# Attention values of four heads in one group every second step, output sums copied by VectorE in the even steps

## The chip, the cores and the metric

The kernel runs on one core of one Trainium2 chip. The metric is the device time of one launch in microseconds (us), as the median of several runs.

## What is computed

One decoder layer, all in float32: self-attention with a causal mask, attention over a context with a mask of its own, and a mixture of experts. Cut to the part that the change touches and what follows it:

```
# x: (2, 256, 256), context: (2, 512, 256), 16 heads of 16, 16 experts, top 4
scores = einsum('bqhd,bkhd->bhqk', Q, K)            # causal: -inf above the diagonal
attn   = softmax(scores)
out    = einsum('bhqk,bkhd->bqhd', attn, V)
x = x + out @ Wo.T + bo
x = x + context_attention(layernorm(x), context, mask)   # zero where no position of the mask is valid
x = x + experts(layernorm(x))
```

## The kernel before

The program is written by hand: each engine has its own instruction list, and semaphores tie the lists together. What follows names TensorE PE, VectorE DVE, ScalarE ACT and GpSimd POOL, as the profile does.

Self-attention runs as a pipeline over 16 steps, v = 0 to 15 (`NV = 16`), and two more that drain it. A step is a pair of heads of one sequence. Two steps make a group `u` of four heads; groups 0 to 3 are the first sequence, 4 to 7 the second. In step v each engine does, in this order:

- **PE**: `scores(v)` (lines 1095 and 1099), then `turn(v-1)`, which transposes the exponentials of the step before (line 1109, three transposes for each of the two heads, each head behind a wait on `exp_done`). In odd steps from 3 on comes `values_first(u)` with u = (v-3)/2 (line 1122): four matmuls of 32 rows of output and 256 queries, over the first block of keys. In the next, even step, after `turn`, comes `values_second(u)` (line 1129), four matmuls over the second block of keys, which ends the sums of the group and increments `av_done`. In two steps, 9 and 17 (`LAST_VALUES`), both parts stand together in the odd step. In the trace each of these f32 matmuls is two instructions, so four are shown as x8.
- **DVE**: in odd steps from 5 on, and in step 10, it first copies the sums of a finished group out of PSUM bank 6 into `osum` (line 812, increments `o_done`). Then it takes the row maxima of the two heads (line 819, four instructions and a short read of the accumulator after each), then copies the first head's transposed exponentials from PSUM to `pt` (line 838). After that stand small pieces of other work: two maxima of the context's mask into `valid` in steps 7 and 8 (line 847); the attention outputs of the first sequence, `outputs` (lines 744 and 745), in steps 10 and 11; `residual` (lines 751 and 657) in steps 12 and 13; `centre` (lines 759, 761, 763) in step 14.
- **ACT**: the exponentials of the step, four activations (line 515), which wait for the maxima, then the second head's copy to `pt` (line 564).

Around the middle other work stands on PE: `turn_back(0, 0)` at the end of step 10 and `turn_back(0, 1)` in step 11 (line 1137), which transpose `osum` of the first sequence back and wait for `o_done` of 4 and, the second, for `att_done`; transposes of `att` (line 1007) at the end of step 11; `project` (line 1146) in step 12; transposes of `xn` in step 15; `context_scores` (line 1158) in steps 16 and 17. POOL makes `pen` (lines 366 and 369) from the mask once both `valid` columns are there, and behind it, on the same engine, the first `rstd` (line 312), which waits for `centre`.

Since `values_first(u)` overwrites the bank that the copy to `osum` reads, it waits for `o_done` of u. PE's `scores(v)` use PSUM banks 2(v mod 3) and the next, so three steps are in flight.

Of the kernel before, what the change touches and what calls it, by code (L numbers as in the profile page):

```python
# [15 lines left out]
B, S, D = 2, 256, 256  # L16
# [10 lines left out]
NG = H // HG  # L27
# [16 lines left out]
def decoder_layer(nc, x_d, ctx_d, ctxT_d, wqkv_d, wo_d, params_d, rows_d, mask_d, dbias_d, we_d, out_d):  # L44
    ctx = ExitStack()
    with ctx:
        def sb(name, shape, dt=F32):
            return ctx.enter_context(nc.sbuf_tensor(name, shape, dt))
# [4 lines left out]
        PS = ctx.enter_context(nc.psum_tensor("PS", [P, 8, 512], F32))  # L53
# [52 lines left out]
        osum = sb("osum", [P, NG, T])  # L106
# [85 lines left out]
        av_done, o_done = sem("av_done"), sem("o_done")  # L192
# [20 lines left out]
        NV = 2 * B * NG  # L213
        Q_BANK = (2, 7)
        TAIL = 2 * NG + 3
        LAST_VALUES = (2 * NG + 1, 4 * NG + 1)

        block = ctx.enter_context(nc.Block())

# [426 lines left out]
        def _(dve):  # L646
            v_ = nc.vector
# [156 lines left out]
            for v in range(NV + 2):  # L804
                if v == 0:
                    dve.wait_ge(causal_done, 2)
                if v == 2 * NG + 2 or (v >= 5 and v % 2 == 1 and v != 2 * NG + 3):
                    u = NG - 1 if v == 2 * NG + 2 else (v - 5) // 2
                    b, hg = divmod(u, NG)

                    dve.wait_ge(av_done, u + 1)
                    v_.tensor_copy(osum[:, hg, b * S:(b + 1) * S], PS[:, 6, 0:S]).then_inc(o_done, 1)  # L812
                if v < NV:
                    for j in range(2):
                        dve.wait_ge(sc_done, 2 * v + j + 1)
                        if v >= 2:
                            dve.wait_ge(exp_done, 2 * v + j - 3)
                        for qc, cols in ((0, slice(0, P)), (1, slice(P, BLK * P))):
                            i = v_.tensor_tensor_reduce(out=masked[:, v % 2, j, cols], in0=PS[:, 2 * (v % 3) + j, cols],  # L819
                                                        in1=causal[:, cols], scale=1.0, scalar=HUGE, op0=ALU.add, op1=ALU.min,  # L820
                                                        accum_out=nmax[:, v % 2, j, qc:qc + 1])
                        i.then_inc(max_done, 1)

                if v == NV - 1:
                    low_tokens(7, yh_done, 1, slice(0, S), yl_done)
                if v == NV:
                    context_scale(0)
                    dve.wait_ge(pen_done, B)
                    context_max(0)
                if v == TAIL:  # L830
                    outputs(0, 1, 7)
                if 1 <= v <= NV and v != NV - 2:

                    w = v - 1
                    dve.wait_ge(pT_done, 2 * w + 1)
                    if w >= 4:
                        dve.wait_ge(av_done, w // 2 - 1)
                    v_.tensor_copy(pt[:, w // 2 % 2, 2 * (w % 2), :, :].rearrange("p c q -> p (c q)"),  # L838
                                   PS[:, 2 * (w % 3), 0:BLK * P]).then_inc(pt_done[0], 1)
                if v == 1:  # L840
                    take_queries(1)
                if v == 5:
                    take_values(1)
                if v in (7, 8):
                    b = v - 7
                    dve.wait_ge(mask_in, 16)
                    v_.tensor_reduce(valid[:, b:b + 1], mask8[:, b * M:(b + 1) * M], AX.X, ALU.max).then_inc(valid_done, 1)
                if v == TAIL - 1:
                    outputs(0, 0, 7)
                if v == TAIL + 1:  # L850
                    dve.wait_ge(xb_done, 1)
                    dve.wait_ge(proj_done, QC)
                    residual(0, 0, PS[:, 7, 0:D])
                if v == TAIL + 2:
                    residual(0, 1, PS[:, 7, D:2 * D])
                if v == TAIL + 3:
                    centre(0)
# [141 lines left out]
        def _(pe):  # L999
# [109 lines left out]
                        i = t.transpose(PS[:, 2 * (v % 3) + j, n * P:(n + 1) * P], pr[:, v % 2, j, n * P:(n + 1) * P], ident[:, :])  # L1109
                    i.then_inc(pT_done, 1)  # L1110

            def values_first(u):

                b, hg = divmod(u, NG)
                if u % NG == 0:
                    pe.wait_ge(v_done, QC * (b + 1))
                for j in range(2):
                    pe.wait_ge(pt_done[j], 2 * u + 2)
                if u >= 1:
                    pe.wait_ge(o_done, u)  # L1120
                for h in range(HG):
                    t.matmul(PS[HP * h:HP * (h + 1), 6, 0:S], vp[:, b * QC, hg * HG + h, :],
                             pt[:, u % 2, h, 0:QC, :].rearrange("p c q -> p (c q)"), start=True, stop=False, skip_group_check=True)

            def values_second(u):

                b, hg = divmod(u, NG)
                for h in range(HG):
                    i = t.matmul(PS[HP * h:HP * (h + 1), 6, P:S], vp[:, b * QC + 1, hg * HG + h, :],
                                 pt[:, u % 2, h, QC, :], start=False, stop=True, skip_group_check=True)  # L1130
                i.then_inc(av_done, 1)
# [59 lines left out]
            for v in range(NV + 2):  # L1191
                if v < NV:
                    scores(v)
                if v == 1:
                    project_heads(0, 1, Q_BANK[1], q_ps)
                if v == 3:
                    pe.wait_ge(q_done, 2 * KD - 1)
                    pe.wait_ge(odd_queries, 1)
                    project_values(1)
                if v == TAIL:  # L1200
                    pe.wait_ge(att_done, 1)
                    turn_back(0, 1, 7)
                if v == TAIL + 1:
                    pe.wait_ge(wo_in, 16)
                    project(0, [PS[:, 7, j * D:(j + 1) * D] for j in range(QC)])
                if v == NV - 1:
                    transposes(xn, 0, 7, xn_done, NC + QC)
                if v == NV:
                    context_scores(0)
                if 1 <= v <= NV:  # L1210
                    turn(v - 1)
                if v == NV + 1:
                    context_scores(1)
                if v >= 3 and v % 2 == 1:
                    values_first((v - 3) // 2)
                if v in LAST_VALUES:
                    values_second((v - 3) // 2)
                if v >= 4 and v % 2 == 0 and v - 1 not in LAST_VALUES:
                    values_second((v - 4) // 2)
                if v == TAIL - 1:  # L1220
                    pe.wait_ge(v_done, NC)
                    turn_back(0, 0, 7)
                if v == TAIL:
                    pe.wait_ge(att_done, QC)
                    transposes(att, 0, 7, att_done, QC)
# [157 lines left out]
```

## Time and profile before

| | us |
|---|---|
| median of 3 runs | 218.23 (218.16 to 218.25) |
| the profiled execution, its own time | 218.16 |
| span of its profile | 216.4 |
| around the span | 1.76 |

Within the span: 0 to 22 us are loads, the first layer norm and the projections with the first attention steps; 22 to 58 us the rest of self-attention; 58 to 84 us the context attention and the router; 84 us to the end the experts, which are a stream of matmuls. The granted TensorE clock is at its full level of 2.4 GHz (1.00) in all of these stretches. A busy engine in the profile need not be at its peak: matmuls are pipelined, their ends are modelled, and rows of the timeline are merged.

### The profile page before, as it was taken

The page shows a single profiled execution, that of the slowest core. Times are in us where ns is not written, and L with a number is a line of the kernel's source. Part 1 is how long each engine was busy: PE and PEld are TensorE (multiplying, and loading weights), DVE is VectorE, ACT ScalarE, POOL GpSimd, SP SyncE. Part 2 cuts the span into 40 slices and gives each one's busy share as a digit, 9 for nine tenths or more (in the row PEclk, how much of TensorE's full clock was granted, in tenths as well). Part 3 has the DMA queues.
Part 4 walks back from the last instruction along what each step waited for, and adds up shares of the span by engine and source line. Part 5 has one row for each costly group of instructions (what it writes and reads, how often), then busy time and mean ns, then how long its engine had stood idle before and what let it go on. Part 6 is the DMA issues. An engine that isn't in the chain of part 4 may idle for free.

```text
span 216.4 us, 4415 instructions
## 1 busy us (share of the span) xinstructions
PE 209.1 (97%) x1392; PEld 174.0 (80%) x1392; DVE 162.7 (75%) x448; ACT 131.1 (61%) x248; POOL 93.9 (43%) x83
## 2 busy tenths in 40 slices
PE   7899999998998999999999999999999999999995
PEld 2687677775686899889889899899898898898893
DVE  3789699778668658888898777686785785786754
ACT  3549898768522614766866676675765666676340
POOL 7799999305002010247535733623614615516000
PEclk9999999999999999999999999999999999999999
DMA  5995430000000000022452144043042142110002
GB/s 166 331 386 183 145 101 2 3 2 3 0 0 0 3 2 0 0 75 75 145 148 79 67 145 145 1 145 128 17 145 92 53 145 64 82 48 0 0 0 98
DMA packets 8062, 17.45 MB, mean 81 GB/s; under 512 B 960, under 2 KB 3184, under 8 KB 7920
## 3 DMA queue, kind: packets, MB, share of 16 engines
q1 hardware_dynamic: 7616, 16.97, 23.9%
q10 hardware_dynamic: 432, 0.31, 0.5%
q8 instruction: 7, 0.11, 0.2%
q14 instruction: 7, 0.06, 0.1%
HBM read 16.75 MB, written 0.52 MB: 80 GB/s over the span
## 4 chain that ended last, share of the span: by engine, by line
PE 76%; DVE 13%; ACT 3%; issue 3%; DMA 2%; POOL 1%; SPq 0%; DVEq 0%; ACTq 0%
PE PS L1294 35%; PE PS L1310 20%; DVE masked L819 4%; PE PS L1173 3%; PE PS L1158 3%; DMA wqkv<-wqkv_d 2%; PE PS L1146 2%; PE PS L1109 2%; PE PS L1339 2%; ACT pr L515 1%; PE PS L1261 1%; PE PS L1095 1%; DVE pt L838 1%; DVE osum L812 1%; PE PS L1167 1%
## 5 line engine op out<-in xcount | busy, mean ns | idle before, releaser
L343 POOL TENSOR_TENSOR WLg<-raw_g,WHg 128x1024 fp32r<-128x1024 f32 x16 | 38.5, 2406 | 68.3 <-ACT WHg L475 68.1
L1294 PE MATMUL PS<-XH,WHg 128*128 128x512 f32 x120 | 47.0, 391 | 0.0
L1294 PE MATMUL PS<-XL,WHg 128*128 128x512 f32 x120 | 46.9, 391 | 0.0
L1294 PE MATMUL PS<-XH,WLg 128*128 128x512 f32 x120 | 46.7, 389 | 0.0
L945 DVE TENSOR_SCALAR pt<-pt 128x512 f32<-128x512 f32 x30 | 23.7, 790 | 20.8 <-ACT pt L608 20.8
L1310 PE MATMUL PS<-WHd,HH 128*128 128x256 f32 x120 | 34.0, 283 | 0.2 <-DVE HL L954 0.2
L1310 PE MATMUL PS<-WLd,HH 128*128 128x256 f32 x120 | 34.0, 283 | 0.0
L1310 PE MATMUL PS<-WHd,HL 128*128 128x256 f32 x120 | 33.9, 283 | 0.0
L614 ACT ACTIVATE HH<-pt 128x512 fp32r<-128x512 f32 x30 | 18.9, 630 | 18.0 <-DVE pt L949 18.0
L608 ACT ACTIVATE pt<-PS,bup 128x512 f32<-128x512 f32 x30 | 20.7, 689 | 13.4 <-PE PS L1294 13.4
L515 ACT ACTIVATE pr<-masked,nmax 128x128 f32<-128x128 f32 x64 | 23.8, 448 | 7.0 <-DVE nmax L819 5.5
L949 DVE SCALAR_TENSOR_TENSOR pt<-pt 128x512 f32<-128x512 f32 x30 | 24.9, 831 | 4.2 <-DVE pt L945 1.4
L1294 PEld LDWEIGHTS PS<-XH,WLg 128*128 128x128 f32 x120 | 22.6, 188 | 4.8
L605 ACT ACTIVATE pt<-PS,params 128x512 f32<-128x512 f32 x30 | 20.6, 687 | 9.4 <-PE PS L1294 9.4
L1294 PEld LDWEIGHTS PS<-XH,WHg 128*128 128x128 f32 x120 | 22.6, 188 | 4.3
L1294 PEld LDWEIGHTS PS<-XL,WHg 128*128 128x128 f32 x120 | 22.6, 188 | 4.1
L938 DVE SCALAR_TENSOR_TENSOR x<-PS,score,x 128x256 f32<-128x256 f32 x60 | 24.8, 476 | 0.0
L1310 PEld LDWEIGHTS PS<-WHd,HH 128*128 128x128 f32 x120 | 23.0, 191 | 0.9 <-DVE HL L954 0.4
L1310 PEld LDWEIGHTS PS<-WHd,HL 128*128 128x128 f32 x120 | 23.0, 191 | 0.5
L1310 PEld LDWEIGHTS PS<-WLd,HH 128*128 128x128 f32 x120 | 23.0, 191 | 0.0
L954 DVE TENSOR_TENSOR HL<-pt,HH 128x512 fp32r<-128x512 f32 x30 | 20.7, 689 | 1.5
L819 DVE CUSTOM_DVE_ANT_0 masked<-PS,causal 128x128 f32<-128x128 f32 x64 | 18.9, 353 | 2.6 <-PE PS L1099 2.5
(196 smaller groups left out, 371.4 us busy)
## 6 DMA issues: line engine op xcount, KB each, us to landing
raw_g<-we_d SPq DMA_DIRECT2D x16, 512.0 KB, 4.0
raw_w<-we_d SPq DMA_DIRECT2D x16, 256.0 KB, 2.7
ctxT<-ctxT_d SPq DMA_DIRECT2D x1, 1024.0 KB, 10.3
ctx_sb<-ctx_d SPq DMA_DIRECT2D x1, 1024.0 KB, 12.3
wqkv<-wqkv_d SPq DMA_DIRECT2D x3, 256.0 KB, 4.7
out_d<-x SPq DMA_DIRECT2D x4, 128.0 KB, 1.8
rows<-rows_d SPq DMA_DIRECT2D x1, 264.0 KB, 6.2
x<-x_d ACTq DMA_DIRECT2D x2, 128.0 KB, 3.1
```

Source lines behind the costliest of these rows:

```text
L343: g.tensor_tensor(WLg[slot][:, :, :, :].rearrange("p k g f -> p (k g f)"), raw_g[slot][:, :], WHg[slot][:, :, :, :].rearrange("p k g f -> ...
L515: i = a.activation(pr[:, v % 2, j, cols], masked[:, v % 2, j, cols], ACT.Exp, bias=nmax[:, v % 2, j, qc:qc + 1], scale=-1.0)
L605: a.activation(glu[:, m, :], PS[:, 2 * m, :], ACT.Gelu_apprx_sigmoid, bias=gub[:, bass.ds(e, 1), 0, m]).then_inc(glu_done, 1)
L608: a.activation(upc[:, m, :], PS[:, 2 * m + 1, :], ACT.Identity, bias=bup1[:, bass.ds(e, 1), m]).then_inc(up_done, 1)
L614: a.activation(HH[slot][:, m, :], hid[:, m, :], ACT.Copy).then_inc(hh_done, 1)
L819: i = v_.tensor_tensor_reduce(out=masked[:, v % 2, j, cols], in0=PS[:, 2 * (v % 3) + j, cols], in1=causal[:, cols], scale=1.0, scalar=HUGE ...
L938: v_.scalar_tensor_tensor(out=acc[:, c, :], in0=PS[:, 4 + 2 * slot + c // 2, (c % 2) * D:(c % 2 + 1) * D], scalar=score[:, c, bass.ds(e, 1 ...
L945: v_.tensor_scalar(upc[:, m, :], upc[:, m, :], 1.0 - LIMIT, 1.0 + LIMIT, ALU.max, ALU.min).then_inc(upc_done, 1)
L949: v_.scalar_tensor_tensor(out=hid[:, m, :], in0=glu[:, m, :], scalar=GLU_MAX, in1=upc[:, m, :], op0=ALU.min, op1=ALU.mult).then_inc(hid_do ...
L954: v_.tensor_tensor(HL[slot][:, m, :], hid[:, m, :], HH[slot][:, m, :].bitcast(F32), ALU.subtract).then_inc(hl_done, 1)
L1294: i = t.matmul(PS[:, 2 * m + part, :], w[slot][:, k, part, m * P:(m + 1) * P], xx[:, k, :], start=(n == 0), stop=(n == 3 * KD - 1))
L1310: i = t.matmul(PS[:, 4 + 2 * slot + c // 2, (c % 2) * D:(c % 2 + 1) * D], hh[slot][:, k, c * P:(c + 1) * P], w[slot][:, k, :], start=(n == ...
```

## The change

Both parts of a group's values now stand in one function, `values(u)`, called in each odd step v = 2u + 3. `LAST_VALUES` is gone. DVE copies the sums of groups 0 to 6 in the even steps v = 2u + 4, after the maxima and ahead of the copy to `pt`; ACT still copies group 7. The two maxima of the mask move from steps 7 and 8 to steps 10 and 12. No instruction is added or removed.

```diff
                 if v == 0:
                     dve.wait_ge(causal_done, 2)
-                if v == 2 * NG + 2 or (v >= 5 and v % 2 == 1 and v != 2 * NG + 3):
-                    u = NG - 1 if v == 2 * NG + 2 else (v - 5) // 2
-                    b, hg = divmod(u, NG)
-
-                    dve.wait_ge(av_done, u + 1)
-                    v_.tensor_copy(osum[:, hg, b * S:(b + 1) * S], PS[:, 6, 0:S]).then_inc(o_done, 1)
                 if v < NV:
...
                         i.then_inc(max_done, 1)
 
+                if v >= 4 and v % 2 == 0 and v <= NV:
+                    u = (v - 4) // 2
+                    b, hg = divmod(u, NG)
+
+                    dve.wait_ge(av_done, u + 1)
+                    v_.tensor_copy(osum[:, hg, b * S:(b + 1) * S], PS[:, 6, 0:S]).then_inc(o_done, 1)
...
-                if v in (7, 8):
-                    b = v - 7
+                if v in (10, 12):
+                    b = (v - 10) // 2
                     dve.wait_ge(mask_in, 16)
                     v_.tensor_reduce(valid[:, b:b + 1], mask8[:, b * M:(b + 1) * M], AX.X, ALU.max).then_inc(valid_done, 1)
...
-            def values_first(u):
+            def values(u):
...
-
-            def values_second(u):
-
-                b, hg = divmod(u, NG)
                 for h in range(HG):
                     i = t.matmul(PS[HP * h:HP * (h + 1), 6, P:S], vp[:, b * QC + 1, hg * HG + h, :],
...
                 if v >= 3 and v % 2 == 1:
-                    values_first((v - 3) // 2)
-                if v in LAST_VALUES:
-                    values_second((v - 3) // 2)
-                if v >= 4 and v % 2 == 0 and v - 1 not in LAST_VALUES:
-                    values_second((v - 4) // 2)
+                    values((v - 3) // 2)
```

The first place is PE from the transposes of step 4 to the values of step 5. Before:

```order
L1109 MATMUL PS<-ident,pr 128x128 x6
L1129 MATMUL PS<-pt,vp 32x128 x4
L1095 MATMUL PS<-kT,qpar 128x128 x2
L1099 MATMUL PS<-HH 128x256 x2
L1099 MATMUL PS<-HH,HL 128x256 x2
L1099 MATMUL PS<-HL,HH 128x256 x2
L1109 MATMUL PS<-ident,pr 128x128 x6
L1122 MATMUL PS<-pt,vp 32x256 x4
```

After, the same place on PE:

```order
L1108 MATMUL PS<-ident,pr 128x128 x6
L1094 MATMUL PS<-kT,qpar 128x128 x2
L1098 MATMUL PS<-HH 128x256 x2
L1098 MATMUL PS<-HH,HL 128x256 x2
L1098 MATMUL PS<-HL,HH 128x256 x2
L1108 MATMUL PS<-ident,pr 128x128 x6
L1121 MATMUL PS<-pt,vp 32x256 x4
L1124 MATMUL PS<-pt,vp 32x128 x4
```

The four short matmuls went from between the transposes and the scores to behind the four long ones.

The second place is DVE in step 10, where the last group of the first sequence is finished. `masked,nmax` with `nmax` are the maxima, `rsum` and `att` are `outputs(0, 0)`. Before:

```order
L812 COPY osum<-PS 128x256
L819 ISA masked,nmax<-PS,causal 128x128
L819 ISA nmax 128x1
L819 ISA masked,nmax<-PS,causal 128x256
L819 ISA nmax 128x1
L819 ISA masked,nmax<-PS,causal 128x128
L819 ISA nmax 128x1
L819 ISA masked,nmax<-PS,causal 128x256
L819 ISA nmax 128x1
L838 COPY pt<-PS 128x384
L744 RECIPROCAL rsum<-PS 128x16
L745 TENSOR_TENSOR att<-PS,rsum 128x256
```

After, from the last of the same maxima on DVE:

```order
L812 ISA masked,nmax<-PS,causal 128x256
L812 ISA nmax 128x1
L822 COPY osum<-PS 128x256
L837 COPY pt<-PS 128x384
L846 TENSOR_REDUCE valid<-mask 128x1
L743 RECIPROCAL rsum<-PS 128x16
L744 TENSOR_TENSOR att<-PS,rsum 128x256
```

The copy of the sums went from ahead of the maxima to behind them, and the mask's maximum stands ahead of the outputs.

The third place is DVE from the last maximum of step 12 to the first of step 13, where `x<-PS,xb` and `stats` are `residual(0, 0)`. Before:

```order
L819 ISA nmax 128x1
L838 COPY pt<-PS 128x384
L751 TENSOR_TENSOR x<-PS,xb 128x256
L657 BN_STATS stats<-x 128x6
L812 COPY osum<-PS 128x256
L819 ISA masked,nmax<-PS,causal 128x128
```

After, the same place on DVE:

```order
L812 ISA nmax 128x1
L822 COPY osum<-PS 128x256
L837 COPY pt<-PS 128x384
L846 TENSOR_REDUCE valid<-mask 128x1
L750 TENSOR_TENSOR x<-PS,xb 128x256
L656 BN_STATS stats<-x 128x6
L812 ISA masked,nmax<-PS,causal 128x128
```

The copy of the sums moved ahead of the copy to `pt`, and the second maximum of the mask came in ahead of the residual.

## Rows read from the trace of the kernel before

**Rows 1.** Busy us (instructions) by stretch: PE, PEld, DVE, ACT, POOL; clock; DMA.
```profile
22.40:41.00 18.60, 18.33 (x211) 12.89 (x211) 17.42 (x85) 16.07 (x44) 16.77 (x13) 1.00 0.20 66
```

**Rows 2.** Timeline of PE, steps 4 to 6: start, us, what, [idle before].
```profile
22.96 0.49 PE L1095 MATMUL PS<-kT,qpar 32*128 32x128 f32 x4
...
23.73 0.88 PE L1109 MATMUL PS<-ident,pr 128*128 128x128 f32 x6
24.54 0.42 PE L1129 MATMUL PS<-pt,vp 128*32 128x128 f32 x8
24.89 0.49 PE L1095 MATMUL PS<-kT,qpar 32*128 32x128 f32 x4
...
25.67 0.94 PE L1109 MATMUL PS<-ident,pr 128*128 128x128 f32 x6
26.54 0.64 PE L1122 MATMUL PS<-pt,vp 128*32 128x256 f32 x8
27.11 0.49 PE L1095 MATMUL PS<-kT,qpar 32*128 32x128 f32 x4
```

**Rows 3.** Timeline of PE, step 9 (both parts together) and step 10's scores.
```profile
34.90 0.64 PE L1122 MATMUL PS<-pt,vp 128*32 128x256 f32 x8
...
35.69 0.49 PE L1095 MATMUL PS<-kT,qpar 32*128 32x128 f32 x4
```

**Rows 4.** Timeline of DVE, step 4: first maximum, then the copy to pt.
```profile
23.83 0.29 DVE L819 CUSTOM_DVE_ANT_0 masked<-PS,causal 128x128 f32<-128x128 f32 x1 [1.11 <-PE PS L1099]
...
24.95 0.55 DVE L838 COPY pt<-PS 128x384 f32<-128x384 f32 x1
```

**Rows 5.** Timeline of ACT, the four exponentials of step 4.
```profile
24.51 1.50 ACT L515 ACTIVATE pr<-masked,nmax 128x128 f32<-128x128 f32 x4 [0.69 <-DVE nmax L819]
```

**Rows 6.** Timeline of weight loads from 30.3 us: second head's transposes, step 7.
```profile
30.24 0.31 PEld L1109 LDWEIGHTS PS<-ident,pr 128*128 128x128 f32 x3
30.72 0.16 PEld L1122 LDWEIGHTS PS<-pt,vp 128*32 128x32 f32 x8 [0.17 <-issue]
```

**Rows 7.** Timeline of PE, steps 10 to 12.
```profile
37.27 0.60 PE L1137 MATMUL PS<-ident,osum 128*128 128x128 f32 x4
37.80 0.49 PE L1095 MATMUL PS<-kT,qpar 32*128 32x128 f32 x4
...
38.92 0.66 PE L1137 MATMUL PS<-ident,osum 128*128 128x128 f32 x4 [0.27 <-DVE att L745]
...
41.31 0.49 PE L1095 MATMUL PS<-kT,qpar 32*128 32x128 f32 x4
```

**Rows 8.** Timeline of DVE, steps 8 to 10.
```profile
33.75 0.68 DVE L847 TENSOR_REDUCE valid<-mask 128x1 f32<-128x512 uint8 x1
34.34 0.41 DVE L812 COPY osum<-PS 128x256 f32<-128x256 f32 x1
...
38.16 0.25 DVE L744 RECIPROCAL rsum<-PS 128x16 f32<-128x16 f32 x1
38.44 0.42 DVE L745 TENSOR_TENSOR att<-PS,rsum 128x256 f32<-128x256 f32 x1
```

**Rows 9.** Timeline of DVE, steps 12 and 13.
```profile
44.49 0.56 DVE L838 COPY pt<-PS 128x384 f32<-128x384 f32 x1 [1.10 <-PE PS L1109]
...
45.76 0.41 DVE L812 COPY osum<-PS 128x256 f32<-128x256 f32 x1
46.08 0.28 DVE L819 CUSTOM_DVE_ANT_0 masked<-PS,causal 128x128 f32<-128x128 f32 x1
```

**Rows 10.** Timeline of PE: context scores of step 16, the context's first transposes.
```profile
52.62 0.50 PE L1158 MATMUL PS<-keys_high,XH 128*128 128x512 f32 x1 [0.39 <-DVE XL L801]
...
57.60 0.66 PE L1167 MATMUL PS<-ident,qpar 128*128 128x128 f32 x4
...
59.73 0.66 PE L1167 MATMUL PS<-ident,qpar 128*128 128x128 f32 x4 [0.47 <-ACT qpar L522]
```

**Rows 11.** Timeline of POOL: the mask's penalties.
```profile
35.58 4.10 POOL L369 TENSOR_SCALAR pen<-pen,valid 128x512 f32<-128x512 f32 x2
```

More of the change, by code:

```diff
@@ L215, in decoder_layer @@
         TAIL = 2 * NG + 3
-        LAST_VALUES = (2 * NG + 1, 4 * NG + 1)
         block = ctx.enter_context(nc.Block())
```

## The prediction, made before the changed kernel was run

> **What bounds the kernel now.** The busy times by stretch come first [rows 1]. From 22.4 to 41.0 us PE is busy 18.33 of 18.60 us and DVE 17.42, with TensorE's clock at its full level (1.00). Neither has room, so the question is which of them waits for the other inside a step, and that is read from the timelines.
>
> PE's timeline of steps 4 to 6 [rows 2] gives the cost of each piece, from the start of one to the start of the next: scores 0.77 us (22.96 to 23.73), transposes 0.81 (23.73 to 24.54), second part of the values 0.35 (24.54 to 24.89), scores of step 5 0.78, transposes 0.87 (25.67 to 26.54), first part of the values 0.57 (to 27.11). The row of step 5's transposes is 0.06 longer than that of step 4's, though it holds the same six instructions. The reason is in the other engines' rows. Scores that start at 22.96 let DVE start its maxima at 23.83, after an idle wait, 0.87 later [rows 4]; ACT starts the exponentials at 24.51 and ends the fourth at 26.01 [rows 5]. So the exponentials of a step end 3.05 us after PE starts its scores. In step 7 the second head's transposes start at 30.24 and PE goes on at 30.72, 0.48 later [rows 6].
>
> This is a latency that PE covers with other work. Between the start of scores(4) and the second head's transposes of step 4 stand scores 0.77, transposes 0.81, second part 0.35, scores 0.78 and the first head's transposes, 0.35 to 0.40 (half of 0.81, or 0.81 less some 0.46): 3.06 to 3.11 us. That is just the 3.05 plus a few hundredths for the semaphore. The second part of the values in the even step is what fills the time.
>
> **The change, step by step.** I go by PE's shift against its own rows, from scores(4) on.
>
> *Values in one group.* Where both parts already stand together they take 0.79 us (34.90 to 35.69) [rows 3], apart 0.57 + 0.35 = 0.92 [rows 2]. Six groups are merged (two were): 0.13 less each, 0.78 in all. In an odd step PE has 0.22 more, in the next even one 0.35 less. So scores(4), behind values(0), come 0.22 late.
>
> *The latency laid open.* Without the 0.35, PE has only 2.71 to 2.76 us of work to cover 3.05 and some hundredths: the second head's transposes wait 0.32 to 0.37 us in steps 5, 7 and 9. The period of two steps is then 3.08 (scores to the end of the exponentials, with 0.03 for the semaphore) + 0.46 (from the second head's transposes to the values, between 0.40 and the 0.48 of [rows 6]) + 0.79 = 4.33 us. Before, it was 27.11 - 22.96 = 4.15 for the first pair [rows 2], and 35.69 - 27.11 = 8.58 for the next two together [rows 2, 3]. Three periods of 4.33 are 12.99 against 12.73: 0.26 more, with the 0.22 at the start 0.48. Scores(10) start at about 36.17 instead of 35.69. The saved 0.13 is thus more than eaten.
>
> *The two maxima of the mask* leave steps 7 and 8: 0.59 to 0.68 us of DVE each (33.75 to 34.34, or its own 0.68) [rows 8]. This makes DVE early, but PE in these steps now waits for a latency that starts with its own scores, so nothing comes of it.
>
> *Step 10, the largest term.* `turn_back(0, 0)` waits for the copy of group 3's sums. Before, that copy stood ahead of the maxima, and turn_back started at 37.27 straight behind the transposes [rows 7]. Now DVE does it behind the maxima of step 10, and these wait for scores(10). From scores at 36.17: + 0.87 to the first maximum = 37.04, + 1.12 for the four maxima (23.83 to 24.95 [rows 4]) = 38.16, + 0.41 for the copy [rows 8] = 38.57, turn_back at about 38.60. PE had nothing left since 36.17 + 0.77 + 0.81 = 37.75: it idles 0.85 us. Scores(11) follow 0.53 after turn_back (37.27 to 37.80) at 39.13, 1.33 late. Nothing is queued on PE that could pass this wait; behind it stand all scores to come, and DVE and ACT wait for those.
>
> *The mask's maximum in step 10* stands ahead of outputs(0, 0) on DVE, for which turn_back(0, 1) waits. DVE: copy of the sums 38.16, copy to pt 38.49, mask 38.96, outputs 39.56 (step costs 0.33, 0.47, 0.60), attention rows ready 0.70 after (38.16 to 38.86 [rows 8]) = 40.26, turn_back(0, 1) at 40.3 against 38.92: 1.37 late [rows 7]. So it adds 0.04 to the shift here; without it the outputs would wait for turn_back anyway.
>
> *Steps 11 to 13.* Values(4) whole in step 11: + 0.22, scores(12) 1.59 late (41.31 before [rows 7]). DVE's maxima of step 12 shift by the same. The copy of group 4's sums falls into the idle 1.10 us ahead of the copy to pt [rows 9] and costs nothing there; it leaves the place ahead of step 13's maxima, 0.32 less (45.76 to 46.08 [rows 9]). The second mask maximum comes in ahead of the residual, 0.59 more. DVE runs from there without a gap, so step 13's maxima are 1.59 + 0.59 - 0.32 = 1.86 late. PE has its second part no more in step 12 and is only 1.24 late: DVE leads until step 15.
>
> *Steps 14 to 17.* The copy of group 5 now stands ahead of `centre` in step 14, 0.33 more for the transposes of xn, which then are 2.19 late; PE waits for them longer than before. They reach the context scores by ACT's copy and DVE's subtraction, both of which had to come behind the maxima of step 15 before (1.86 late), so the context scores of step 16 (52.62 before, after a wait [rows 10]) are 1.86 to 2.19 late, say 1.95. Step 16 loses its second part on PE, 0.35, the last of the six. The context's first transposes (57.60 [rows 10]) are 1.60 late. From here on PE and what it feeds have their old order.
>
> *The mask's penalties on POOL* take 4.10 us [rows 11] and can start only after step 12, at about 47.3; they end near 51.5. Behind them on POOL stands the rstd that waits for `centre`, and DVE's first maximum over the context needs both, but also PE's scores of step 16, which now start at about 54.6 [rows 10] and take some 1.5 us. Free, with one to three microseconds to spare.
>
> **Sum.** 0.22 + 0.26 + 0.85 + 0.04 + 0.22 + (1.86 - 1.59, the mask's maximum) 0.27 + 0.09 (centre) - 0.35 = 1.60 us. Against the profiled execution's 218.16 that is 219.8; its own time stands 0.07 under the median of 218.23, which changes nothing. Bounds: the wait laid open may be 0.2 or 0.4 in each of the three steps (0.4 either way in the sum), and the way through centre and ACT 0.1 less or 0.24 more.
>
> The Trainium skill, page "TensorEngine Tiling (Array Packing)", section "Tiling Modes", says that changing the tiling mode drains TensorE. By that rule the change takes away one change of mode in each of six groups and should gain. The 0.79 against 0.92 of the rows above agrees in sign; what the rule leaves out is who needs the time in between.
>
> **The rivals.**
> *Faster: PE is bound by its own work.* If the transposes never wait, the merged groups give their full 0.78 and the step-10 wait is short, because DVE, freed of the mask, is early: 217.4. For it speaks PE's 18.33 of 18.60 busy; against it, that 3.05 us from scores to exponentials is a chain that DVE's free time does not shorten. It decides at a latency of 2.75 us or less.
> *About the same: waits that PE has anyway take it up.* PE idles 0.27 at 38.92 [rows 7], 0.39 ahead of the context scores and 0.47 at 59.73 [rows 10], 1.13 in all. If they ended on something that has not moved, that much of the 1.60 would go: 218.6. Against it: they end on DVE's and ACT's work on what PE itself has made just before, so they move along, and the chain of the sum above already says what becomes of the first two.
> *Slower still: POOL.* If the penalties and the rstd behind them come later than the context scores of step 16, at some 56 us, the context's first maximum waits, and each microsecond beyond counts in full. Price, if POOL takes half as long again as its 4.10 us and its small work behind comes as late, up to 1: 220.8. For it: the 4.10 us now lie between step 12 and step 16.
> *The change does not do what it says* can be left out: the order on the engines shows it.
>
> **Chances.** Forecast 0.80, faster 0.05, PE's other waits 0.10 (0.08 of it within the bound of no change), POOL 0.05. The unknown costs make 219.2 to 220.4; I reach down to 218.7, near the case of the other waits, since a step of the chain that is sized too high has more ways than one too low. A measurement of this kernel can tell about 0.2% (0.44 us) from no change: faster 0.05, within 0.08, slower 0.87.
>
> **What would show it.** In the profile after: transposes of steps 5, 7 and 9 with 0.3 us more in their row; PE idle of about 0.85 before line 1132 (turn_back) in step 10, released by DVE's copy to osum; scores(10) half a microsecond late, scores(12) 1.6; the context's first transposes near 59.2; the experts unchanged in length. It is wrong if turn_back in step 10 starts without a wait, if the transposes' rows keep their 0.81 to 0.87, or if the shift at 59.2 is not found at the end.

## The result and the profile after

| | before | changed |
|---|---|---|
| median of 4 runs, us | 218.24 (218.16 to 218.28) | 220.03 (219.53 to 221.23) |
| ratio | | 1.0092, 95% interval 1.0072 to 1.0111 |
| profiled execution, its own time | 218.16 | 219.53 |
| its span | 216.4 | 217.8 |

The changed kernel is slower by 0.9%, with 219.8 forecast. Ratios, here and below, are of executions within 1.5% of their kernel's fastest, which leaves out a single one (221.75 us, of e7). Two things stand in the table that need taking apart. The profiled execution is only 1.37 us longer, and one execution took 221.23, far more than the spread of the kernel before.

The first is a matter of where the clock is started. The loads at the front jitter by some tenths from run to run. A point behind them is PE's `project_values(1)` in step 3, whose first matmul has a row of its own in every timeline; the first transposes of the context attention (57.60 before [rows 10]) are the end of what the change touches. I call the time between them **the stretch**. Its start before, in the timeline of PE, and the transposes of `xn` in step 15:

```profile
20.15 0.39 PE L1070 MATMUL PS<-wqkv_high,XH 128*128 128x256 f32 x1
...
50.31 0.70 PE L1007 MATMUL PS<-ident,xn 128*128 128x128 f32 x4 [0.32 <-DVE xn L763]
```

So the stretch is 57.60 - 20.15 = 37.45 us before. PE's timeline after (start, us, what, idle before in brackets), from that point on:

```profile
19.94 0.38 PE L1069 MATMUL PS<-wqkv_high,XH 128*128 128x256 f32 x1
...
23.00 0.49 PE L1094 MATMUL PS<-kT,qpar 32*128 32x128 f32 x4
...
23.77 0.87 PE L1108 MATMUL PS<-ident,pr 128*128 128x128 f32 x6
24.57 0.49 PE L1094 MATMUL PS<-kT,qpar 32*128 32x128 f32 x4
...
25.41 1.24 PE L1108 MATMUL PS<-ident,pr 128*128 128x128 f32 x6
26.58 0.64 PE L1121 MATMUL PS<-pt,vp 128*32 128x256 f32 x8
27.03 0.40 PE L1124 MATMUL PS<-pt,vp 128*32 128x128 f32 x8
27.36 0.49 PE L1094 MATMUL PS<-kT,qpar 32*128 32x128 f32 x4
...
36.10 0.49 PE L1094 MATMUL PS<-kT,qpar 32*128 32x128 f32 x4
...
38.65 0.63 PE L1132 MATMUL PS<-ident,osum 128*128 128x128 f32 x4 [0.90 <-DVE osum L822]
...
40.24 0.66 PE L1132 MATMUL PS<-ident,osum 128*128 128x128 f32 x4 [0.18 <-DVE att L744]
...
42.86 0.49 PE L1094 MATMUL PS<-kT,qpar 32*128 32x128 f32 x4
...
52.44 0.70 PE L1006 MATMUL PS<-ident,xn 128*128 128x128 f32 x4 [1.01 <-DVE xn L762]
...
54.55 0.50 PE L1153 MATMUL PS<-keys_high,XH 128*128 128x512 f32 x1
...
56.05 0.81 PE L1108 MATMUL PS<-ident,pr 128*128 128x128 f32 x6
56.62 0.48 PE L1153 MATMUL PS<-keys_high,XH 128*128 128x512 f32 x1
...
58.99 0.66 PE L1162 MATMUL PS<-ident,qpar 128*128 128x128 f32 x4
...
61.13 0.66 PE L1162 MATMUL PS<-ident,qpar 128*128 128x128 f32 x4 [0.47 <-ACT qpar L521]
```

The stretch is 58.99 - 19.94 = 39.05 us: **1.60 us longer**. What follows it is 158.8 us in both (217.8 - 58.99, 216.4 - 57.60). The reader is to see four things against [rows 2, 7, 10]: the transposes of step 5 have a row of 1.24 us where it was 0.94; turn_back waits 0.90 us for DVE's copy where it followed without a gap; the transposes of xn wait 1.01 us where it was 0.32; and the wait of 0.39 ahead of the context scores is gone.

The row of 1.24 us hides a wait, which the weight loads of the same transposes show. The exponentials of step 4 on ACT, then the weight loads of the second head's transposes in step 5 (PEld is the weight load of TensorE):

```profile
24.56 1.49 ACT L514 ACTIVATE pr<-masked,nmax 128x128 f32<-128x128 f32 x4 [0.95 <-DVE nmax L812]
...
26.10 0.31 PEld L1108 LDWEIGHTS PS<-ident,pr 128*128 128x128 f32 x3 [0.38 <-ACT pr L514]
```

The exponentials end at 26.05, 3.05 us behind the start of their scores (23.00), and the transposes start at 26.10, released by ACT.

DVE after, steps 10, 12 and 13:

```profile
38.08 0.42 DVE L822 COPY osum<-PS 128x256 f32<-128x256 f32 x1
38.42 0.55 DVE L837 COPY pt<-PS 128x384 f32<-128x384 f32 x1
38.88 0.68 DVE L846 TENSOR_REDUCE valid<-mask 128x1 f32<-128x512 uint8 x1
39.48 0.25 DVE L743 RECIPROCAL rsum<-PS 128x16 f32<-128x16 f32 x1
39.76 0.42 DVE L744 TENSOR_TENSOR att<-PS,rsum 128x256 f32<-128x256 f32 x1
...
46.03 0.56 DVE L837 COPY pt<-PS 128x384 f32<-128x384 f32 x1 [0.77 <-PE PS L1108]
46.51 0.68 DVE L846 TENSOR_REDUCE valid<-mask 128x1 f32<-128x512 uint8 x1
47.10 0.41 DVE L750 TENSOR_TENSOR x<-PS,xb 128x256 f32<-128x256 f32 x1
...
47.90 0.27 DVE L812 CUSTOM_DVE_ANT_0 masked<-PS,causal 128x128 f32<-128x128 f32 x1
```

In the busy times of the window 22.4 to 41.0 us (PE, PEld, DVE, ACT, POOL), against [rows 1], PE falls by 1.24 us and DVE by 1.89. Part of this is work that now lies behind 41.0 us (PE has 197 instructions in the window where it had 211, DVE one maximum of the mask where it had two). But no engine has become busier: the added time is in waits of the engines for one another.

```profile
22.40:41.00 18.60, 17.09 (x197) 12.23 (x190) 15.53 (x80) 14.50 (x40) 12.53 (x10) 1.00 0.19 66
```

The second thing, the executions of 221 us, is taken up in the experiments e4, e6, e10 and e11.

### The profile page after: what moved, and what is told of

Same layout as the page of the kernel before. It is cut to its first block, busy times and chain, and to the rows that moved or that the text cites. A ratio compares the mean times of both kernels' runs of the same rounds, so it can differ in the third digit from the quotient of the medians.

```text
span 217.8 us, 4415 instructions
## 1 busy us (share of the span) xinstructions
PE 209.1 (96%) x1392; PEld 175.0 (80%) x1392; DVE 163.7 (75%) x448; ACT 131.1 (60%) x248; POOL 93.7 (43%) x83
## 4 chain that ended last, share of the span: by engine, by line
PE 82%; DVE 10%; ACT 4%; issue 3%; POOL 0%; DVEq 0%; ACTq 0%; POOLq 0%
PE PS L1285 35%; PE PS L1301 20%; PE PS L1168 3%; PE PS L1153 3%; PE PS L1108 3%; ACT pr L514 2%; PE PS L1022 2%; PE PS L1121 2%; DVE masked L812 2%; PE PS L1141 2%; PE PS L1094 2%; PE PS L1330 2%; PE PS L1006 1%; PE PS L1252 1%; PE PS L1098 1%
## 5 line engine op out<-in xcount | busy, mean ns | idle before, releaser
L944 DVE TENSOR_SCALAR pt<-pt 128x512 f32<-128x512 f32 x30 | 24.8, 828 | 20.5 <-ACT pt L607 20.5
L948 DVE SCALAR_TENSOR_TENSOR pt<-pt 128x512 f32<-128x512 f32 x30 | 24.1, 803 | 4.2 <-DVE pt L944 1.6
```

Of the source, the lines that this page charges most:

```text
L944: v_.tensor_scalar(upc[:, m, :], upc[:, m, :], 1.0 - LIMIT, 1.0 + LIMIT, ALU.max, ALU.min).then_inc(upc_done, 1)
L948: v_.scalar_tensor_tensor(out=hid[:, m, :], in0=glu[:, m, :], scalar=GLU_MAX, in1=upc[:, m, :], op0=ALU.min, op1=ALU.mult).then_inc(hid_do ...
```

## The experiments

Eleven runs. "Stretch" is that of each one's profiled execution; the ratio is to runs of the kernel before on the same chip. Filler means matmuls of zeros (128x512, bf16) whose result nobody reads. The stretch of e11 is of an execution in which TensorE's clock fell.

| | what | median us | ratio (95%) | stretch us |
|---|---|---|---|---|
| | before | 218.2 | | 37.45 |
| | changed | 220.03 | 1.0092 (1.0072 to 1.0111) | 39.05 |
| e1 | before, values in one group | 218.50 | 1.0013 (1.0005 to 1.0022) | 37.83 |
| e2 | before, copy of group 3 late | 219.06 | 1.0035 (1.0022 to 1.0048) | 38.28 |
| e3 | before, mask maxima late | 219.42 | 1.0050 (1.0037 to 1.0063) | 38.60 |
| e4 | changed, again | 220.55 | 1.0108 (1.0081 to 1.0135) | 39.05 |
| e5 | changed, mask maxima early | 219.15 | 1.0036 (1.0023 to 1.0049) | 38.29 |
| e6 | changed, copy of group 3 early | 220.37 | 1.0122 (1.0107 to 1.0138) | 38.71 |
| e7 | changed, both put back | 218.39 | 1.0006 (0.9997 to 1.0015) | 37.58 |
| e8 | before, maxima in step 3, group 6 merged | 217.62 | 0.9975 (0.9965 to 0.9984) | 36.97 |
| e9 | e1 with filler in steps 4, 6, 8 | 218.52 | 1.0018 (1.0009 to 1.0027) | 37.84 |
| e10 | changed, filler in step 15 | 219.70 | 1.0072 (1.0059 to 1.0085) | 39.03 |
| e11 | changed, filler in step 10 | 220.53 | 1.0104 (1.0082 to 1.0127) | 40.28 |

### e1: the values alone

```diff
-        LAST_VALUES = (2 * NG + 1, 4 * NG + 1)
+        LAST_VALUES = range(3, NV + 2, 2)
```

> The kernel before with both parts of each group's values together in the odd step, copies and mask maxima where they were. Theory A (a latency laid open: scores to end of exponentials 3.08 us, PE's own work between them only 2.7): the transposes of steps 5, 7 and 9 take 0.3 to 0.4 us longer, scores(10) starts 0.4 to 0.5 us later than 35.69, and some of it is taken up by waits that follow: 0.3 to 0.5 us slower at the end (218.5 to 218.7). Theory B (PE bound by its own work, one change of tile shape less per group): the transposes keep 0.87 us and the kernel is 0.4 to 0.8 us faster.

The stretch grew by 0.38 us, and the median is 0.23 above the before of the same chip, 0.1% by the ratio, not faster. Theory A had 0.3 to 0.5 at the end. PE's timeline of e1 has the long row in step 5 (and the same 1.24 in steps 7 and 9):

```profile
24.51 0.87 PE L1109 MATMUL PS<-ident,pr 128*128 128x128 f32 x6
...
26.15 1.24 PE L1109 MATMUL PS<-ident,pr 128*128 128x128 f32 x6
```

Scores(10) start 16.17 us into the stretch, 15.54 before: 0.63 late, more than the 0.4 to 0.5 expected. Theory B is out. That the 0.37 us in the row is a wait in which PE could do other work is tested by e9.

### e9: filler in the place of the values

```diff
                     values_second((v - 4) // 2)
+                if v in (4, 6, 8):
+                    for j in range(2):
+                        pe.wait_ge(pt_done[j], v - 1)
+                    keep_warm(2 * ((v + 1) % 3), 1)
```

> The kernel of e1 (values in one group, nothing else moved) with one matmul of zeros, 128x512 bf16, about 0.22 us, put on PE behind the transposes of steps 4, 6 and 8, where the second part of the values stood. It adds work that the reference does not need; the output is unchanged. Theory A (PE waits 0.37 us for the exponentials in steps 5, 7 and 9): the filler goes into that wait, scores(10) start 16.2 us after project_values(1) as in e1 (16.17), and the stretch stays at 37.8 to 37.9 us. Theory B (PE is bound by its own work there): 0.22 us more in each of the three pairs, scores(10) at 16.8, the stretch 38.5.

The filler costs nothing: scores(10) at 16.17 us, stretch 37.84 against 37.83. It went into the row of the transposes, 1.08 instead of 1.24:

```profile
25.93 1.08 PE L1109 MATMUL PS<-ident,pr 128*128 128x128 f32 x6
```

PE has free time there, and the period of two steps, 4.36 to 4.41 us in e1 and in e9, is set by the way from scores to exponentials. That is the same latency of 3.05 us of [rows 2, 5].

### e2: the copy of group 3 alone

```diff
-                if v == 2 * NG + 2 or (v >= 5 and v % 2 == 1 and v != 2 * NG + 3):
+                if (v >= 5 and v % 2 == 1 and v != 2 * NG + 3):
...
                         i.then_inc(max_done, 1)
+                if v == 2 * NG + 2:
+                    dve.wait_ge(av_done, NG)
+                    v_.tensor_copy(osum[:, NG - 1, 0:S], PS[:, 6, 0:S]).then_inc(o_done, 1)
```

> The kernel before with only group 3's copy to osum moved from ahead of the maxima of step 10 to behind them. Theory A (the sum of the prediction: the wait of turn_back in step 10 is 0.7 to 0.85 us and all of it reaches the end): turn_back starts near 38.0 instead of 37.27, and the kernel is 0.7 us slower. Theory B (the step 10 wait partly takes the place of the 0.27 us wait for the attention rows that followed it): the wait is there, but only 0.4 to 0.55 us reach the end.

```profile
38.34 0.63 PE L1140 MATMUL PS<-ident,osum 128*128 128x128 f32 x4 [0.81 <-DVE osum L826]
38.89 0.49 PE L1098 MATMUL PS<-kT,qpar 32*128 32x128 f32 x4
39.77 0.66 PE L1140 MATMUL PS<-ident,osum 128*128 128x128 f32 x4
```

The wait of 0.81 us is there. The wait of 0.27 at the second turn_back [rows 7] is gone, but the stretch is still 0.83 us longer, so theory A has it: moved alone, one copy of 0.4 us costs 0.8.

### e3: the mask maxima alone

```diff
-                if v in (7, 8):
-                    b = v - 7
+                if v in (10, 12):
+                    b = (v - 10) // 2
```

> The kernel before with only the two mask maxima moved to steps 10 and 12. Theory A (the prediction's sum, where they cost 0.3 us): 0 to 0.3 us slower. Theory B (both stand on the path that ends: ahead of the attention rows in step 10, for which turn_back waits, and ahead of the residual in step 12, from which DVE leads to the context scores): 0.9 to 1.1 us slower, turn_back(0, 1) near 39.4, context scores of step 16 near 53.6 instead of 52.62.

This is where my sum had the weights wrong. The two maxima alone make the stretch 1.15 us longer, more than the copy and a little more than theory B's 0.9 to 1.1. PE's timeline of e3:

```profile
39.82 0.65 PE L1137 MATMUL PS<-ident,osum 128*128 128x128 f32 x4 [0.96 <-DVE att L745]
...
54.11 0.50 PE L1158 MATMUL PS<-keys_high,XH 128*128 128x512 f32 x1 [0.39 <-DVE XL L801]
```

The maximum of step 10 makes turn_back(0, 1) wait 0.96 instead of 0.27 us; scores(12) are then 0.56 us late. The context scores are 1.15 late (33.62 us into the stretch, 32.47 before), so that the other 0.59 comes with the maximum of step 12, which shifts the residual and all that DVE does behind it. That is the 0.59 that one maximum takes on DVE [rows 8].

### e5, e6, e7: the changed kernel with parts put back

e5 puts the mask's lines back as they were (the diff of e3, reversed), e6 the copy of group 3:

```diff
+                if v == 2 * NG + 2:
+                    dve.wait_ge(av_done, NG)
+                    v_.tensor_copy(osum[:, NG - 1, 0:S], PS[:, 6, 0:S]).then_inc(o_done, 1)
                 if v < NV:
...
-                if v >= 4 and v % 2 == 0 and v <= NV:
+                if v >= 4 and v % 2 == 0 and v <= NV and v != 2 * NG + 2:
```

e7 does both.

> The changed kernel with the two mask maxima back in steps 7 and 8. From PE's project_values(1) to the context's first transposes the kernel before takes 37.45 us and the changed one 39.05. Theory A (the prediction's sum, the maxima cost 0.3 us of the 1.6): 38.7. Theory B (the second maximum, ahead of the residual, makes DVE lead to the context scores; without it the wait of 0.39 us ahead of those takes up part of the other terms): 38.1 to 38.2, the kernel 0.9 us faster than the changed one, waits of 0.9 us in step 10 unchanged.

> The changed kernel with only group 3's copy to osum put back ahead of the maxima of step 10. Theory A (the step 10 wait of 0.90 us is the largest term and all of it reaches the end): 38.2 us for the stretch that takes 39.05 in the changed kernel and 37.45 before. Theory B (the mask's maximum ahead of the attention rows holds turn_back(0, 1) nearly as long): turn_back(0, 0) starts without a wait, the wait moves to turn_back(0, 1), and 38.6 to 38.8 us remain. If the 0.90 us wait is also what lets the granted clock fall in some executions, none of them shows a mean clock of 0.992 here.

> The changed kernel with the mask maxima and group 3's copy both put back: what is left is the values in one group and the other copies in even steps. Theory A (latency laid open, three waits of 0.3 to 0.4 us, less what later waits take up): 37.6 to 37.9 us for the stretch that takes 37.45 before, the kernel 0.2 to 0.4 us slower than before. Theory B (PE bound by its own work once these are away): 36.7 us, the kernel 0.7 us faster than before.

Without the late maxima (e5) the stretch is 38.29, 0.76 less than the changed kernel's (near theory B's 38.2); without the late copy (e6) 38.71, only 0.34 less (theory B); without both (e7) 37.58, 1.47 less (theory A, at its lower end). The parts are not additive: e1, e2 and e3 alone give 0.38 + 0.83 + 1.15 = 2.36 us, the changed kernel 1.60. Of this difference 0.25 is no overlap: e7 has the merged groups of e1 and the other copies in even steps, and its stretch is shorter than e1's (37.58 against 37.83), so those copies gain something where they now stand. The other 0.51 is overlap. The reason shows in e6's row of the second turn_back. With the first one no longer waiting, PE waits for the attention rows instead, behind the mask's maximum:

```profile
40.02 0.66 PE L1135 MATMUL PS<-ident,osum 128*128 128x128 f32 x4 [0.94 <-DVE att L744]
```

Copy and maximum delay the same thing, the second turn_back, and either alone is enough for most of it: against before it is 0.76 us late with the copy alone (e2), 0.56 with the maxima alone (e3), and with both the changed kernel is 0.89 later than e7. e7's other copies in even steps and its merged groups cost 0.13 us, and its time cannot be told from that of before (interval 0.9997 to 1.0015): it is 0.87 late at scores(12), 0.66 at the context scores, where 0.39 of waiting is gone, and step 16 gives back 0.53.

### e4, e10, e11: the executions of 221 us

> The changed kernel once more, to see whether its times always spread over 1.7 us (219.5 to 221.2) where the kernel before spreads over 0.1 us. Theory A (the shift is all: 1.4 us by the profile): median near 219.6, spread under 0.3. Theory B (something further happens in some executions, such as a stretch at the lower TensorE clock): spread over 0.5 us again, and the executions above 220 show a mean granted clock under 1.00.

Of six executions three took 221.2 us with a mean granted clock of 0.992, three 219.5 to 219.9 with 0.999 or 1.000: the spread of 1.8 us is theory B's. With the first four (221.23 at 0.992 among them) that is four in ten. e6 had three in six (220.6 to 221.2); e1, e2, e3, e5, e8 and e9 had none, and no run of the kernel before; of e7's twelve one stood out (221.75 us, mean clock 0.984), with no trace of it; its clock lost twice as much and its time over twice as much as in the others, so it may be another event at another place. Something happens to TensorE's clock. It is not brought by the wait of 0.90 us in step 10, as e6's expectation asked: e6 does not have that wait, and e5 has one of 0.77 there and no such execution. (e6's 0.94 at the second turn_back stands alike in e3, 0.96, which has none either.) The two kernels that had it share the late maxima together with merged groups, and both idle 1.01 us ahead of the transposes of xn in step 15, where e5 and e7 idle 0.81, e1 and e9 0.69 and e3 0.33. e10 and e11 put work into one wait each:

```diff
                 if v == NV - 1:
+                    pe.wait_ge(max_done, 2 * (NV - 2) + 2)
+                    keep_warm(4, 4)
                     transposes(xn, 0, 7, xn_done, NC + QC)
```

```diff
                     pe.wait_ge(v_done, NC)
+                    for j in range(2):
+                        pe.wait_ge(pt_done[j], 9)
+                    keep_warm(4, 4)
                     turn_back(0, 0, 7)
```

> The changed kernel with four matmuls of zeros (128x512 bf16, some 0.9 us) on PE in step 15, where it idles 1.01 us ahead of the transposes of xn. They are work that the reference does not need. Theory A (the executions of 221.2 us with a mean granted clock of 0.992 come from PE doing little around step 15, where e4 and e6 idle 1.0 us and e5 and e7 0.8): the stretch keeps 39.0 to 39.2 us and no execution shows 0.992; all lie near 219.6 to 220.1. Theory B (they come from elsewhere): about half of the executions show 0.992 and 221 us again.

> The changed kernel with four matmuls of zeros (128x512 bf16, some 0.9 us) on PE in step 10, where it idles 0.90 us ahead of turn_back(0, 0). They are work that the reference does not need. Theory A (the place is step 15, not step 10): the stretch keeps 39.0 to 39.2 us and executions at 0.992 appear as in e4. Theory B (step 10's wait is the place): none appears here, and they appear in e10.

e10 and e11 ran on the same chip. e10's five executions (its filler ran from 51.89, behind a wait of 0.29) lie between 219.61 and 219.93, none with a lower clock. e11 had three of six at 0.992, and its profiled execution was one of them, so the place can be read (theory A of both). PE's last row before the wait, and busy times with the clock behind them (PE, PEld, DVE, ACT, POOL, clock):

```profile
51.39 0.29 PE L1098 MATMUL PS<-HL,HH 32*128 32x256 f32 x2
...
52.00:52.20 0.20, 0.00 (x0) 0.00 (x0) 0.18 (x3) 0.20 (x2) 0.00 (x0) 0.97 0.00 0
52.20:52.40 0.20, 0.00 (x0) 0.00 (x0) 0.19 (x2) 0.20 (x2) 0.00 (x0) 0.50 0.00 0
52.00:54.00 2.00, 1.31 (x6) 1.31 (x7) 1.97 (x14) 1.56 (x5) 1.43 (x3) 0.55 0.00 0
54.00:56.00 2.00, 2.00 (x22) 1.20 (x20) 1.16 (x3) 2.00 (x6) 1.34 (x2) 0.60 0.00 0
56.00:58.00 2.00, 2.00 (x18) 1.62 (x11) 0.59 (x3) 0.19 (x1) 0.00 (x0) 1.00 0.04 8
```

The clock fell to its lower level, 1.2 GHz (0.50), in the wait of step 15, at 52.2 us, when PE had been idle for half a microsecond, and was back at 2.4 GHz before 56 us. PE's timeline of e11 there shows the price:

```profile
52.69 1.11 PE L1006 MATMUL PS<-ident,xn 128*128 128x128 f32 x4 [1.01 <-DVE xn L762]
53.60 1.49 PE L1108 MATMUL PS<-ident,pr 128*128 128x128 f32 x6
55.02 0.90 PE L1121 MATMUL PS<-pt,vp 128*32 128x256 f32 x8
...
60.50 0.66 PE L1162 MATMUL PS<-ident,qpar 128*128 128x128 f32 x4
```

1.49 us for six transposes that take 0.82 in the changed kernel's step 15, 1.11 for the four of xn instead of 0.70; the stretch is 40.28, 1.23 us longer than 39.05. The place is shown by e11's trace. That PE's idling there is the cause rests on e10, whose filler stands just there: had each of its executions the chance of the three kernels without it (the changed one, e6, e11: 10 of 22), five without a fall would come by chance once in twenty times. The length of this wait cannot be the whole of it, since the clock fell half a microsecond into it and e5 and e7 idle 0.81 there. What else sets them apart in the traces is step 14: the changed kernel, e6 and e11 have there one more row of 1.24 us with its hidden wait of 0.37, e5 and e7 have 0.87. No run changes the one without the other, so which of the two counts stays open.

### e8: a version that beats both

```diff
-        LAST_VALUES = (2 * NG + 1, 4 * NG + 1)
+        LAST_VALUES = (2 * NG + 1, 4 * NG - 1, 4 * NG + 1)
...
+                if v == 3:
+                    take_mask(0)
                 if 1 <= v <= NV and v != NV - 2:
...
-                if v in (7, 8):
-                    b = v - 7
-                    dve.wait_ge(mask_in, 16)
-                    v_.tensor_reduce(valid[:, b:b + 1], mask8[:, b * M:(b + 1) * M], AX.X, ALU.max).then_inc(valid_done, 1)
+                if v == 3:
+                    take_mask(1)
```

> A version meant to beat both: the kernel before with the two mask maxima in step 3 on DVE, where it idles 0.72 and 1.11 us, and the values of group 6 alone merged (step 15, where the transposes of xn and the context scores cover the exponentials' latency). Theory A: group 6's second part leaves step 16, where it was on the path: 0.35 us less; the mask maxima leave steps 7 and 8: 0.1 to 0.2 us less; 36.9 to 37.1 us for the stretch of 37.45, the kernel 0.4 to 0.5 us faster than before. Theory B (PE waits less but later waits take it up): within 0.2 us of before.

217.62 us, 0.25% faster than before (0.9965 to 0.9984); the stretch is 36.97, 0.48 less, as theory A had it. It also starts its context scores behind a wait of 0.17 us where it was 0.39, since the second part of group 6 now stands there. The maxima stand where DVE idled, between the scores of step 3 and those of step 4:

```profile
21.11 0.68 DVE L806 TENSOR_REDUCE valid<-mask 128x1 f32<-128x512 uint8 x1
...
22.42 0.68 DVE L806 TENSOR_REDUCE valid<-mask 128x1 f32<-128x512 uint8 x1
...
23.62 0.29 DVE L823 CUSTOM_DVE_ANT_0 masked<-PS,causal 128x128 f32<-128x128 f32 x1 [0.52 <-PE PS L1103]
```

DVE still waits 0.52 us for step 4's scores: both are free. But up to the context scores the stretch gained only 0.02 (32.45 us into it, 32.47 before); the rest came behind them, from group 6's second part leaving step 16. So theory A's 0.1 to 0.2 for the maxima was not found: scores(10) and scores(12) start 0.02 us earlier than before, no more. Two things were changed at once, so this is read from the rows and not from a run of its own.

## Why the prediction was right, step by step

The forecast was 1.60 us, the stretch gave 1.60, and the waits stood where the prediction put them. That the figure is exact is partly luck, as the steps show. Shifts are against before, from the start of the stretch.

| | predicted | measured |
|---|---|---|
| scores(10) | +0.48 | +0.62 (16.16 - 15.54) |
| wait ahead of turn_back(0, 0) | 0.85 | 0.90 |
| turn_back(0, 0) | +1.33 | +1.59 (18.71 - 17.12) |
| turn_back(0, 1) | +1.37 | +1.53 (20.30 - 18.77) |
| scores(12) | +1.59 | +1.76 (22.92 - 21.16) |
| maxima of step 13 | +1.86 | +2.03 (27.96 - 25.93) |
| context scores of step 16 | +1.95 | +2.14 (34.61 - 32.47) |
| context's first transposes | +1.60 | +1.60 |

**The latency laid open** was right in kind and 0.14 us too small. The period of two steps was put at 4.33 and is 4.37 (27.36 - 23.00 = 4.36 in the rows above), since the way from the second head's transposes to the values takes the whole 0.48 of [rows 6], not 0.46 (26.10 to 26.58), and the semaphore 0.05, not 0.03. That makes 0.11 in three periods; the other 0.03 is there at the start, where scores(4) are 0.25 late and not 0.22. The weight load released by ACT and e9 show that it is a wait. The long row is 1.24 against the 0.87 of an even step: 0.37, within the 0.32 to 0.37 of the text. (The text's bound of 0.4 either way for the three waits does not follow from its own 0.2 to 0.4 in each: that is some 0.45 less or 0.15 more. Nothing hung on it.)

**Step 10**: the wait was right to 0.05 us. The shift that it brings was 0.12 too small: turn_back(0, 0) starts 2.55 us behind scores(10) (38.65 - 36.10) where it was 1.58, so 0.97 later and not 0.85, because it starts 0.15 us behind the end of the copy and not 0.03. Of this the second turn_back takes some back, its wait going from 0.27 to 0.18. But the text called it the largest term, with the mask's maximum behind it adding only 0.04. This was a way of counting, not a property of the kernel. In the order in which the chain meets them, the copy comes first and takes the delay; the maximum, which would have made the same turn_back late, finds little left. Taken out alone, the copy is worth 0.34 us (e6) and the two maxima 0.76 (e5: scores(12) come 0.17 earlier, where the text had 0.04 for the first maximum, and the rest comes behind); put in alone, 0.83 (e2) and 1.15 (e3). Someone who had used my list to repair the kernel would have started with the wrong part.

**Steps 12 to 15** were right but for the 0.17 us that they inherit: the maximum ahead of the residual makes DVE lead, with 2.03 - 1.76 = 0.27 as forecast, and the copy of group 4 falls into an idle time (1.10 before, 0.77 of it left [rows 9]). The transposes of xn are 2.34 us late (2.19 forecast). The context scores are 0.2 less late than these, since the 0.39 us of waiting ahead of them is now filled by the second part of the values.

**Step 16** was the term that was mis-sized the other way: 0.35 us for the missing second part. In PE's timeline of before, the transposes of step 16 and the context scores of step 17 are

```profile
54.12 0.82 PE L1109 MATMUL PS<-ident,pr 128*128 128x128 f32 x6
54.87 0.43 PE L1129 MATMUL PS<-pt,vp 128*32 128x128 f32 x8
55.22 0.50 PE L1158 MATMUL PS<-keys_high,XH 128*128 128x512 f32 x1
```

with 1.10 us from one to the other for transposes and values; now it is 56.05 to 56.62, 0.57: 0.53 saved. The second part itself is 0.35 of it; the other 0.18, which the prediction put at nothing, is in the transposes, which took 0.75 us up to the values and take 0.57 up to the context scores. The 0.19 too much here cancels the 0.19 that was too little ahead, and this is luck.

**POOL** was free, as forecast: the penalties started at 47.37, took the 4.10 us of [rows 11], and the rstd behind them still waited 0.74 us for `centre`:

```profile
47.37 4.10 POOL L368 TENSOR_SCALAR pen<-pen,valid 128x512 f32<-128x512 f32 x2 [12.12 <-DVE valid L846]
52.21 0.76 POOL L311 TENSOR_TENSOR rstd<-ve,half 128x2 f32<-128x2 f32 x1 [0.74 <-DVE ve L760]
```

**The rival of PE's own work** is out by e1 and e9, **that of waits that take it up** is out in its main term, the wait at 61.13 (0.47, as before), which moved along; of the other two 0.09 and 0.39 are gone, and the stretch is 1.60 us longer all the same. **What no rival had** is the clock: the six executions of the changed kernel without the fall (first four and e4 together) have a median of 219.9, as 218.24 + 1.60 would give; with the others the medians are 220.03 and, in e4, 220.55.

## What to carry to other kernels

A piece of work on a saturated engine may be what covers another chain's latency: before merging it elsewhere, add up what the engine has left between starting that chain and needing its result (here 2.7 us against 3.1). A copy or a reduction that costs nothing by its size costs its whole way to the consumer when it is queued behind something that waits, so place small work in an idle time of its own engine, ahead of nothing that is waited for (e8). And list the delays of a change by taking each out alone as well as by adding each: the terms of a chain sum depend on their order.

## What the runs showed of the hardware that was not expected

- **The clock fell in a wait of one microsecond.** The changed kernel and its relatives idle 1.01 us in step 15, and in 10 of their 22 executions the mean granted clock of TensorE was 0.992. The one of these with a trace (e11) shows the clock at 1.2 GHz from half a microsecond into that wait, costing 1.2 us of the stretch. With four matmuls of zeros in the wait it fell in none of 5. Of the seventeen executions of e5 and e7, with 0.81 us at that place, one had a lower mean clock. What PE did before the wait differs too (step 14), and what exactly counts stays open.
- **A change of the array's shape cost 0.1 to 0.2 us here.** In step 16, six transposes (128x128) take 0.75 us up to values (128x32) before (54.12 to 54.87), and 0.57 up to context scores of their own full shape after (56.05 to 56.62). The first part of the values (128x32) takes 0.57 us up to scores (32x128) before (26.54 to 27.11 [rows 2]), and 0.45 up to the second part, of its own shape, after (26.58 to 27.03). The Trainium skill, page "TensorEngine Tiling (Array Packing)", section "Tiling Modes", says that a change of mode drains TensorE: the trace agrees in sign, with 0.18 and 0.12 us in these two places. That the drain is all of the difference is not shown, since another instruction follows in each pair.
